# Edge features of two tiles stacked on 128 rows, against a block-diagonal weight

## The reference

```
e   = edge_attr @ We                      # [E, 64] @ [64, 128]
k_j = k[src] + e ;  v_j = v[src] + e
logits = sum(q[dst] * k_j, per head) / 4
alpha  = softmax of logits over the edges of one dst
agg    = sum over those edges of alpha * v_j
```

## Time and profile before

| | us |
|---|---|
| median of 3 runs | 2039.2 (2037.81 to 2045.62) |
| the profiled execution | 2027.35 |
| its span, first to last instruction | 2025.6 |

### The profile page before, as it was taken

One profiled execution on the slowest core, in us unless ns is written; L12 is line 12 of the kernel. 1 busy time (PEld: TensorE's weight loads), 2 busy tenths in 40 slices (PEclk: granted clock), 3 DMA queues, 4 the chain that ended last, 5 costly groups with the idle time before them and its releaser, 6 DMA issues.

```text
span 2025.6 us, 34439 instructions
## 1 busy us (share of the span) xinstructions
PE 1301.3 (64%) x8024; PEld 1095.5 (54%) x8025; DVE 1196.7 (59%) x2701; ACT 858.3 (42%) x2586; POOL 960.0 (47%) x1012
## 2 busy tenths in 40 slices
PE   2726666565656566689835666757667675767592
PEld 1325556455645565569335565646556564656382
DVE  5416655655656556744415676766767666677646
ACT  1403545554445445535401445344444534344442
POOL 1273555665656556220171545555555645554062
PEclk9857777777777877759866877878777777868696
DMA  6332233323332333200132333333333333331001
GB/s 136 106 110 62 82 95 94 99 87 90 95 94 87 90 94 100 58 0 0 67 115 63 92 102 96 100 106 94 99 95 98 99 93 107 88 104 56 0 0 32
DMA packets 78615, 166.50 MB, mean 82 GB/s; under 512 B 26149, under 2 KB 41042, under 8 KB 78373
## 3 DMA queue, kind: packets, MB, share of 16 engines
q0 software_dynamic: 39936, 109.11, 19.0%
q1 hardware_dynamic: 36127, 54.38, 8.8%
q10 hardware_dynamic: 2438, 1.89, 0.3%
HBM read 156.56 MB, written 8.75 MB: 82 GB/s over the span
## 4 chain that ended last, share of the span: by engine, by line
PE 34%; DVE 27%; another core or an unknown queue 20%; issue 13%; POOL 1%; DVEq 1%; ACT 1%; DMA 1%; SPq 0%; ACTq 0%; POOLq 0%
PE PS L661 7%; PE PS L662 6%; DVE KV L935 4%; PE PS L714 4%; DVE PR L942 3%; DVE OH L1025 3%; DVE Ls L949 3%; PE PS L640 3%; PE PS L797 3%; PE PS L672 3%; PE PS L788 2%; DVE KV L1040 2%; PE PS L696 1%; POOL KV L419 1%
## 5 line engine op out<-in xcount | busy, mean ns | idle before, releaser
L419 POOL DMA_INDIRECT KV<-kv_table,idx x832 | 879.2, 1057 | 788.8 <-issue 341.6
L661 PE MATMUL PS<-QT,OHT 128*128 x1664 | 419.0, 341 | 109.6 <-issue 78.4
L662 PE MATMUL PS<-QT,OHT 128*128 x1664 | 392.6, 325 | 10.4 <-issue 10.3
L661 PEld LDWEIGHTS PS<-QT,OHT 128*128 128x128 f32 x1664 | 329.2, 246 | 122.6 <-issue 119.3
L549 ACT ACTIVATE AGG<-AGG,PC,RCS x832 | 321.0, 386 | 53.8 <-issue 41.5
L662 PEld LDWEIGHTS PS<-QT,OHT 128*128 128x128 f32 x1664 | 324.5, 242 | 8.0 <-issue 8.0
L714 PE MATMUL PS<-OH,KV 128*128 128x128 f32 x1664 | 249.9, 298 | 18.0 <-ACT AGG L549 7.2
L541 ACT ACTIVATE PC<-PS 128x4 f32<-128x4 f32 x208 | 36.1, 173 | 504.1 <-PE PS L714 350.8
L714 PEld LDWEIGHTS PS<-OH,KV 128*128 128x128 f32 x1664 | 225.2, 210 | 24.0 <-issue 21.7
L545 ACT ACTIVATE AGG<-PS 128x127 f32 x832 | 219.1, 263 | 39.1 <-issue 33.7
L935 DVE TENSOR_TENSOR KV<-KV,PS 128x1024 f32<-128x1024 f32 x104 | 125.6, 1208 | 179.8 <-remote 140.8
(11 more groups left out here) (164 smaller groups left out, 1608.3 us busy)
## 6 DMA issues: line engine op xcount, KB each, us to landing
REL<-rel_dram SPq DMA_DIRECT2D x52, 512.0 KB
KV<-kv_table,idx POOLq DMA_INDIRECT x832
EA<-in_edge_batch SPq DMA_DIRECT2D x52, 256.0 KB
kv_table<-KV SPq DMA_DIRECT2D x52, 128.0 KB, 1.7
X<-in_x SPq DMA_DIRECT2D x2, 832.0 KB, 11.5
GATES<-edge_gates SPq DMA_DIRECT2D x8, 208.0 KB, 8.3
out<-Y SPq DMA_DIRECT2D x2, 448.0 KB
idx<-in_src_batch SPq DMA_DIRECT2D x52, 8.0 KB, 1.6
```

The source lines that it names most:

```text
L419: g.indirect_dma_start(KV[:, s, j, :], None, kv_table, bass.IndirectOffsetOnAxis(ap=idx[:, s, j:j + 1], axis=0)).then_inc(gathered[s][hh], 16)
L661: te.matmul(o, OHT[:, q // 2, 0, e0:e0 + P], QT[:, ds(blk, P)], start=True, stop=False)
L662: last = te.matmul(o, OHT[:, q // 2, 1, e0:e0 + P], QT[:, ds(blk + P, P)], start=False, stop=True)
```

## The change

Tiles are taken in pairs. EA becomes 128 rows by 8 x 128: rows 0 to 63 hold the features of the even tile of a pair, rows 64 to 127 those of the odd one. The host lays `edge_batch` out accordingly, so each of the two loads per batch writes 128 rows of 512 numbers where it wrote 64 rows of 1024. We becomes 128 by 256 with the weights in two diagonal blocks and zeros elsewhere; GpSimd zeroes it first, and ScalarE's DMA queue waits for that and loads the weights twice. One matmul then gives 256 columns, 128 for each tile of the pair, so `edge_part` has two in place of four. The scratch rows that lay in EA move to Y.

```diff
-        EA = sb("EA", [ED, J * P])
+        EA = sb("EA", [2 * ED, J // 2 * P])
-        We = sb("We", [ED, D])
+        We = sb("We", [2 * ED, 2 * D])
-        bias_lo = EA[0:3, 0:448].bitcast(BF16)
-        bias_rest = EA[0:3, 448:448 + 896]
+        bias_lo = Y[0:3, 512:960].bitcast(BF16)
+        bias_rest = Y[0:3, 960:960 + 896]
...
-        last_dst = EA[0:G, 1344:1360].bitcast(I32)
+        last_dst = Y[0:G, 1900:1916].bitcast(I32)
...
-                    sp.dma_start(EA[:, hh * 8 * P:(hh + 1) * 8 * P], a["edge_batch"][ds(n, 1), :, hh * 8 * P:(hh + 1) * 8 * P]
+                    sp.dma_start(EA[:, hh * 4 * P:(hh + 1) * 4 * P], a["edge_batch"][ds(n, 1), :, hh * 4 * P:(hh + 1) * 4 * P]
...
+            g.memset(We[:, :], 0.0).then_inc(S["we_zeroed"], 1)
             g.memset(ones[:, :], 1.0).then_inc(S["consts_made"], 1)
...
-            w(We[:, :], a["L1_gnn_We"])
+            act.wait_ge(*done("we_zeroed", 1))
+            for b in range(2):
+                w(We[b * ED:(b + 1) * ED, b * D:(b + 1) * D], a["L1_gnn_We"])
...
-                    for m in range(4):
-                        e0 = (4 * q + m) * P
-                        last = te.matmul(PS[2 + q % 2][:, m * P:(m + 1) * P], EA[:, e0:e0 + P], We[:, :], start=True, stop=True)
+                    for m in range(2):
+                        e0 = (2 * q + m) * P
+                        last = te.matmul(PS[2 + q % 2][:, 2 * m * D:2 * (m + 1) * D], EA[:, e0:e0 + P], We[:, :], start=True, stop=True)
...
-WEIGHTS = 10
+WEIGHTS = 11
...
-        "edge_batch": np.ascontiguousarray(edges.reshape(G, J * P, ED).transpose(0, 2, 1)),
+        "edge_batch": np.ascontiguousarray(edges.reshape(G, J // 2, 2, P, ED).transpose(0, 2, 4, 1, 3)).reshape(G, 2 * ED, J // 2 * P),
```

More of the change, by code:

```diff
@@ L154, in build @@
         count_rows, same_rows = PS[4][0:TP, 0:T], PS[5][0:TP, 0:T]
-        last_dst = EA[0:G, 1344:1360].bitcast(I32)
-        prev_dst = EA[0:G, 1360:1376].bitcast(I32)
-        same_tile = EA[0:G, 1376:1392]
-        gate_rows = EA[0:G, 1392:1392 + ROW]
+        last_dst = Y[0:G, 1900:1916].bitcast(I32)
+        prev_dst = Y[0:G, 1916:1932].bitcast(I32)
+        same_tile = Y[0:G, 1932:1948]
+        gate_rows = Y[0:G, 1948:1948 + ROW]
         tiles = lambda x: x.rearrange("p (k e) -> p k e", k=TK)
@@ L169, in build @@
             rel_loaded gate_loaded out_stored""".split()}
-        counts = """consts_made rel_made gate_made prep_step kv_copied kv_free gates_made loops_step seen_step
+        counts = """we_zeroed consts_made rel_made gate_made prep_step kv_copied kv_free gates_made loops_step seen_step
             pool_go sp_go stat_step moment_step var_ready sd_ready rs_ready
```

## The result

The changed kernel takes 1986.45 us (median of 4 runs, 1979.89 to 1991.94) against 2039.18 us: a ratio of 0.9734, 95% interval 0.9697 to 0.9771. The forecast was 1993. The profiled execution took 1988.19 us, its span is 1986.5 us, the mean granted clock 0.777 of full speed. TensorE's matmul time fell from 1301.3 to 1241.7 us and L675 (the L672 of before; lines of the loops are three further down) has 416 records of 256 columns.

A forecast was written before the change was run, and what follows sets the result against it. The prediction took a TensorE-VectorE chain in the second layer's edge loop, with VectorE waiting for late-finishing matmuls, as the bound. 48 us gained minus 2 lost gave 2039 - 46 = 1993 us; range 1966 to 2046, 1966 to 2010 for the forecast case.

The forecast's parts named there:

- The bound: Second layer's edge loop: neither TensorE nor VectorE is full; a chain passing between them sets the 32.3 us round.
- from wait to round: Edge loop: a shorter VectorE wait shortens the round in full or more, 1.4 us less wait with 2.4 less round.
- So the plain matmul time gives nothing: Free stretches, quarter 0: wide matmuls at most 0.28 us against 0.248 for two narrow, filled rows unpriced; +2 us in all.
- 2.2 us: VectorE's wait at L935 for quarter 2's edge part shrinks this much per round, over 22 rounds 48 us.
- my low bound of 1.45 per round: Quarter 2's wait: least saving in us, from four matmuls at the coarser pace of 1.07 us each.
- the price of 0.72 us each: Slow stretch of quarter 2: eight L672 need 5.74 us, taken as a cost per instruction; four would need 2.87.
- rival A: Quarter 2's wait stays, its cost being per column or byte, or its end the gather's: 2041 us, chance 0.28.
- unchanged at 3.6: VectorE's wait ahead of L972 in each layer-2 round was expected to stay at 3.6 us.
- The sum: Whole kernel: 48 us gained at quarter 2 minus 2 lost in matmul time, 46 us less.
- Loads and start: Load of EA and setup of We: hidden behind other work, priced at nothing; without cover the start is +0.9 us.
- Rival B: Saved wait returns larger at quarters 0 and 1 or L808 during the second gathers: 2065 us; 0.13 together with Rival C.
- Rival C: Wide matmuls hide weight loads worse in free stretches, costing 16 us: 2055 us; its chance folded into Rival B's.

The follow-up runs named there:

- experiment 1: Changed kernel with its stacked layout, but every edge product 128 columns wide, four per quarter: 2032.47 us, ratio 0.9939 to the kernel before.
- Experiment 2: Changed kernel with 128-column products in quarter 2 alone: 2031.15 us, ratio 0.9914 to the kernel before.
- experiment 4: Changed kernel with both products of quarter 2 only 128 columns wide, the edge part of its second and fourth tile left out: 1996.06 us, ratio 0.974.
- experiment 3: Changed kernel without the second of quarter 2's two products, the edge part of its third and fourth tile left out: 1965.7 us, ratio 0.9614.
- experiment 9: The changed kernel itself, unaltered, on a third chip where the kernel before takes 1628.21 us: 1612.9 us, ratio 0.9896.
- Experiments 5 to 8, 10 and 12: Quarter 2 ahead of the query products (changed kernel 1.0044, 1.0063; kernel before 1.0187), or six of eight layer-2 gathers left out (changed 0.9721, 0.973; before 0.9895).
- the early quarter: Edge part of quarter 2 moved ahead of the query products: changed kernel 1.0044 and 1.0063, kernel before 1.0187, all on faster chips.

## Why the prediction was right, and where it was not

**The bound.** The chain of VectorE's waits per round, and "from wait to round", held: the waits changed by 35.8 us, VectorE's work by 2.0 and the rounds by 37.9. What the rounds lost beyond the 24.1 us of quarter 2 was other waits, not a factor on this one: over all waits the factor is 1.06.

**"So the plain matmul time gives nothing", +2 us.** Wrong in sign. The bound of 0.28 us per wide record came from 512 columns; measured is 1.73 / 8 = 0.216, less than the 0.248 of the two it replaces. Of that 0.248 a part is the step between row counts; within the group two narrow records take 0.223, so the width itself gives next to nothing. And the sentence that filled against idle rows "differ by too little to matter" passed over the 0.10 us between the groups in the earlier trace rows (1.16 against 1.06): it is the price of the step, 0.29 us for each visit to 64 rows. At quarter 0 the wait fell by 8.1 us. From 1150 to 1750 us it is 0.61 us per round before, 0.39 in experiment 1 and 0.24 in the changed kernel: three fifths of it came with the layout.

The Trainium skill, TensorE: Matmul & The Clock Gate, section Step-by-step: what each phase is for, says of the weight load that its time scales with the columns and that the row count doesn't matter. The trace agrees: the weight loads of L672 with 64 rows have a median of 188 ns, those of L714 with 128 rows 192. The 0.29 us of experiment 1 are lost elsewhere, where the row count changes between neighbours, and of that the sentence says nothing.

**"2.2 us" per round at quarter 2, 48 us.** The mechanism held, the size didn't. That the cost is per instruction is shown by experiments 2 and 4. The wait fell from 4.15 to 3.05 us per round (67.1 / 22): 24 us in place of 48, under my low bound of 1.45 per round. The step that failed is the price of 0.72 us each, the same for every instruction. By the sum of the two waits the last four of eight records cost 1.5 us (7.8 to 6.3), 0.4 each. The last two of four cost at least 2.7 (6.3 to 3.6), at least 1.3 each, since with two records VectorE's own work is the floor. What makes the price fall so isn't shown. In both kernels the starts cluster, at the gather's end or 1.4 us behind it. That near the gather's end the backlog clears faster, a part of rival A, is possible but not shown: the gather's start is itself released by this chain (`agg_ready`), so a fixed distance from its end would show anyway. In experiment 3 most starts lie 2.9 or 4.1 us ahead of that end.

**L972 "unchanged at 3.6".** It fell to 3.12, worth 10.3 us. This is no gain beside the one at quarter 2, but the other part of it. Experiment 2 keeps quarters 0, 1 and 3 wide, and with quarter 2 narrow the sum of the two waits is back at 8.1 us, that of experiment 1, where all are narrow (3.3 + 4.8 us against 3.6 + 4.6). So the records of quarter 2 set the sum, and what divides it between the two waits isn't shown. Taken so, the term was worth 34.4 us, 1.56 per round, at the low bound and not under it.

**The sum.** 24.1 + 10.3 + 8.1 - 4.7 = 37.8 us where 46 were forecast. The 48 us came out as 34.4 (quarter 2 and L972), and the 8.1 at quarter 0, where I had a loss of 2, made up for part of it. The loop gave less than forecast and the medians, 52.7 us apart, gave more; that 1993 came within 7 us is in part luck.

**Loads and start.** Nothing, as priced: the first round begins at 1112.60 against 1112.72, so layer 0 did not move either.

**Rival A** (0.28): its form by column or byte falls with experiment 4, its form by a fixed end with experiment 3. The rule cited for it, in the Trainium skill, Perfetto Trace Analysis, section Tensor Engine Instruction, was read in the prediction as making the bytes matter; experiment 4 decides against that reading. That the semaphore comes after the recorded end is as that page has it, here by 3.6 us at L689. **Rival B**: VectorE's waits after have none ahead of L811, and quarter 0 waits less; it did not happen. The place that the prediction held safe, quarter 3, judged by its records' end, waits once in the changed kernel (1.8 us) and in 17 of 20 rounds of experiment 3 (11.7 us): the late finish counts there too. **Rival C**: the wide records are faster in the free stretches, so it falls; of the groups of eight on the chain all but the last take 1.73 us.

**Open.** Whether the late finish is caused by the gathers. It is seen while they run, but experiment 9 shows the same gathers without it, so at the least something else of that chip is needed. Experiments 5 to 8, 10 and 12, which were to decide it, ran where the lateness is absent. Nor is it known what the early quarter does on the slower chip, nor whether the number of matmuls or that of weight loads counts.

## What to carry to other kernels

Count instructions, not columns, in any stretch where an engine that waits for TensorE starts microseconds after the matmul's recorded end: on the chip that had such a place, four records fewer in it were worth about three times as much as the layout. Fill the 128 rows of the stationary operand, the one that is loaded into the array, where neighbours have 128; a visit to 64 rows cost 0.29 us. Sum all waits of the engine that closes the loop, before and after, and its busy time: when the two differences make up that of the time, as here within 0.1 us, nothing is left to look for on it. And read waits of one line by what they wait for: in experiment 3 those ahead of L938 looked like quarter 2's and were mostly those of its neighbours.

## What was not expected of the hardware

The same kernel takes 2046.4 us on one chip and 1628.8 and 1628.2 on two others. In the second layer's edge loop nearly the whole difference of 136.0 us is VectorE's waits (133.5), those for matmuls that are long over by the records. Of the 376.1 us between the two spans 236.6 lie ahead of that loop and were not taken apart; layer 0 too has remote waits on the slower chip (76.2 us ahead of L945, 47.8 ahead of L975, 47.7 ahead of L811 from 90 to 900 us). Other rows hardly differ between the two profiles of the changed kernel: a gather instruction takes 1051 ns in both, its queue holds 19.0% of 1986.5 us (377) in the one and 23.0% of 1610.4 us (370) in the other, the product at L945 677 and 675 ns. The granted clock of the loop is 0.78 on the one and 0.85 on the other. It is not what makes the matmuls late: in the stretch of the two waits itself it is 1.00 on both, from 1395.4 to 1403.7 us on the one and from 1053 to 1059 on the other.

A gain read from such waits is therefore a gain of that chip: 2.7% there, 1.0% on the one other chip where the changed kernel ran.
